# Two graph transformer layers: scores, segment softmax and sums from three blocks into one loop over four chunks

## The chip, the cores and the metric

The kernel runs on one core of a Trainium2 chip. A core has five engines that run their own instruction streams and meet at semaphores: TensorE (PE, matrix products, with weight loads shown apart as PEld), VectorE (DVE), ScalarE (ACT), GpSimd (POOL) and SyncE (SP). The metric is the device time of one execution in microseconds; lower is better.

## The reference, cut to what matters

A graph of N = 3125 nodes and 50000 edges, D = 128 features, passes through a relational layer, a convolution with batch norm, a GATv2 layer with a feed-forward part, and two transformer layers (`L3`). The last two are what the change rebuilds. H = 4 heads of C = 32:

```python
q = (x @ Wq + bq).reshape(N, H, C); k = ...; v = ...
alpha = jnp.einsum('ehc,ehc->eh', q[dst], k[src]) / jnp.sqrt(jnp.float32(C))
amax = jax.ops.segment_max(alpha, dst, num_segments=N)
ealpha = jnp.exp(alpha - amax[dst])
denom = jax.ops.segment_sum(ealpha, dst, num_segments=N)
attn = ealpha / denom[dst]
out = jax.ops.segment_sum(attn[..., None] * v[src], dst, num_segments=N)
return out.reshape(N, H * C) + x @ Ws + bs
```

## The kernel before, in words

The nodes lie in W = 25 windows of Q = 125. An early stage sorts the edges by destination into PAIRS = 416 pairs of a window and a tile of 128 edges, so that all edges of a pair point into one window. G = 4 pairs make a group, 104 groups in all. `pair_src` and `pair_dst` hold source row and place in the window of each edge, `pair_win_i` the window of each pair; TensorE and its weight-load queue read it into registers (line 892) to address `acc` and the PSUM sums.

A transformer layer is a chain of five blocks, and no engine enters a block before all have left the one before:

- `conv_nodes` makes q, k, v and the skip term for all nodes in `acc` and stores k and v to `kv_table` in DRAM.
- `conv_scores` runs over the groups. GpSimd gathers 128 rows of k and v per pair (line 917, eight groups of buffers `got`, one gather per pair). VectorE makes a one-hot of destinations (line 927), TensorE transposes it (line 1801), ScalarE copies it out as `hot_t` (line 1787), TensorE multiplies it with the window's q (line 1814) into one of two banks `q_b`. VectorE multiplies with k (`prod`, line 1775), reduces over a head (`score`, line 1778) and scales into `alpha` (line 1780). SyncE stores the v half to `v_rows`.
- `segment_softmax` takes all 416 x 4 columns of `alpha` at once: transposes, scans for the running maximum of a segment forward and backward, two products that spread a lane's border value, elementwise passes, and the exponential.
- `conv_sums` runs over 52 double groups: rows of v come back from `v_rows`, VectorE makes one-hots (line 1064) and weighted messages (line 1068), TensorE adds them into seven PSUM banks (line 1092), and the denominators from weights split into three bfloat16 parts (line 1093), with a product of zeros after every second pair (line 1097).
- `conv_finish` divides, adds the skip term and, in the last layer, normalises and stores.

Four lines of TensorE's part in conv_scores set its order, a transpose of the next group ahead of this group's products:

```python
turn(1 - b, g + 1)
pe.wait_ge(copied_t, g + 1)
pe.wait_ge(used, g + 1)
for j in range(G):
```

The code as a program prints it, with the line numbers of the profile:

Of the kernel before, what the change touches and what calls it, by code (L numbers as in the profile page):

```python
# [16 lines left out]
ENG = mybir.EngineType  # L17
# [3 lines left out]
Q, W = 125, 25  # L21
P = 128
# [8 lines left out]
YS, Y_EARLY, SL = 6, 6, 24  # L31
# [5 lines left out]
assert TILES * P >= E and FULL + W <= PAIRS and Q * W == N  # L37
# [51 lines left out]

def nodes(ap):  # L90
    return ap.rearrange("(w q) d -> q w d", q=Q)


def segment_softmax(nc, m, acc=None):
# [3 lines left out]
    with ExitStack() as ctx:  # L98
# [12 lines left out]
        alpha = m.alpha[:, :, :].rearrange("l h p -> l (h p)")  # L111
# [34 lines left out]
        def _(dve):  # L146
# [12 lines left out]
            link(v.tensor_copy(topf, high[:, 0:cols]))  # L159
# [18 lines left out]
            link(v.tensor_tensor(less, m.alpha[:, :, :], top[:, :, :], ALU.subtract))  # L178
# [7 lines left out]
def common(m, sb):  # L186
# [14 lines left out]
    m.alpha = sb("alpha", [P, H, PAIRS])  # L201
# [307 lines left out]
def relation_layer(nc, m, y_table):  # L509

    with ExitStack() as ctx:  # L511
# [19 lines left out]
        same = m.alpha  # L531
        pens = m.small[:, :, :].rearrange("l p k -> l (p k)")
        start_pen, end_pen = (pens[:, k * H * PAIRS:(k + 1) * H * PAIRS].rearrange("l (h p) -> l h p", h=H) for k in range(2))
# [32 lines left out]
        def _(dve):  # L566
# [69 lines left out]
            for h in range(H):  # L636
                go(v.tensor_copy(start_pen[:, h, :], ps[2][:, 0:PAIRS]))
                go(v.tensor_copy(end_pen[:, h, :], ps[3][:, 0:PAIRS]))
# [22 lines left out]
            go(v.tensor_scalar(m.leader[:, :], start_pen[:, 0, :], -1.0, None, ALU.is_lt))  # L661
# [69 lines left out]
        def _(pe):  # L731
# [40 lines left out]
            for k, pen in enumerate((start_pen, end_pen)):  # L772
                flat = pen[:, :, :].rearrange("l h p -> l (h p)")
# [61 lines left out]
def gcn_nodes(nc, m, ins, t_table):  # L835

    with ExitStack() as ctx:
# [4 lines left out]
        tb, hb = [bank(f"t1{i}") for i in range(2)], [bank(f"h1{i}") for i in range(4)]  # L842
        loaded, chain, var_ready, std_ready, x_ready = (sem(n) for n in ("loaded1", "chain1", "var1", "std1", "x1_ready"))
# [3 lines left out]
        @block.sync  # L847
        def _(sp):
            sp.dma_start(w1[:, :], ins["L1_gnn_W"]).then_inc(loaded, 16)
            for w in range(0, W, 5):  # L850
                sp.wait_ge(t_ready, w + 5)
                sp.dma_start(nodes(t_table)[:, w:w + 5, :], tmp[:, w:w + 5, :]).then_inc(stored, 16)
            sp.wait_ge(stored, 16 * (W // 5))

# [8 lines left out]

        @block.scalar
        def _(act):
            std_of(nc, act, stats, var_ready, std_ready, 1)
# [6 lines left out]
        def _(pe):  # L873
            pe.wait_ge(x_ready, 1)
# [130 lines left out]


def conv_sums(nc, m, v_rows):


    with ExitStack() as ctx:  # L1010
        sb, sem, bank = scope(nc, ctx)
        zeros = sb("zeros", [P, 512], BF16)
        rows = sb("rows", [P, 2, WG, D])
        hot = sb("hot", [P, 2, WG, Q])
        msg = sb("msg", [P, 2, WG, D])
        wts = sb("wts", [P, 2, WG, H])
        hot_b, wts3 = sb("hot_b", [P, 2, WG, Q], BF16), sb("wts3", [P, 2, WG, 3, H], BF16)
        left, zero = sb("left", [P, 2, WG, H]), sb("zero", [P, WG, H])
        sums = bank("sums", (P, 8 * 512))
        dens = 7 * 512  # L1020
        used, zeroed, done, hot_ready, wts_ready, msg_ready = (sem(n) for n in (
            "used", "zeroed", "all_summed", "hot_ready", "wts_ready", "msg_ready"))
        hot_b_ready, parts_ready, chain, zero_ready = (sem(n) for n in ("hot_b_ready", "parts_ready", "parts_chain", "zero_ready"))
        come = [sem("come0"), sem("come1")]
        steps = PAIRS // (2 * WG)
        block = ctx.enter_context(nc.Block())


        @block.sync
        def _(sp):  # L1030
            with sp.Fori(0, steps) as i:
                for b in range(2):
# [891 lines left out]
```

## Time and profile before

| what | value |
|---|---|
| median of 3 runs | 4879.6 us (4878.93 to 4885.05) |
| the profiled execution's own time | 4863.76 us |
| its span | 4862.0 us, 67990 instructions |
| PE busy | 3211.9 us (66%) |
| DVE busy | 2813.1 us (58%) |
| POOL busy | 2734.6 us (56%) |
| ACT busy | 888.8 us (18%) |
| mean granted clock of TensorE | 0.716 |

The span runs from the first to the last instruction of the program. Busy shares are averages over stages of different limits; the two transformer layers are the last 1700 us or so. The granted clock is given as a share of 2.4 GHz, so 0.50 is the 1.2 GHz level and 1.0 the 2.4 GHz level. The trace shows a float product as two instructions ("halves"), and one matmul of the program's order is two rows' worth of count there.

### The profile page before, as it was taken

What the parts mean: (1) busy time and instruction counts of PE and PEld (TensorE: products, weight loads), DVE (VectorE), ACT (ScalarE), POOL (GpSimd) and SP (SyncE); (2) the same over time, 40 slices, a digit from 0 to 9 for tenths busy, and PEclk for the clock granted to TensorE, in tenths of its full rate; (3) what the DMA queues carried; (4) which work ended last, traced back from release to release, by engine and by line L of the source; (5) the groups of instructions that cost most, each with busy time, mean ns of one, the idle gap of its engine ahead of it and who ended that gap; (6) DMA issues with size and microseconds to landing.
All of it is one profiled execution on the core that took longest, in us unless ns stands there. A gap on an engine that the chain in (4) does not pass through costs nothing. (4 is left out here: it accounts for less than half of the span.)

```text
span 4862.0 us, 67990 instructions
## 1 busy us (share of the span) xinstructions
PE 3211.9 (66%) x15577; PEld 2186.9 (45%) x15578; DVE 2813.1 (58%) x9606; ACT 888.8 (18%) x2002; POOL 2734.6 (56%) x3193
## 2 busy tenths in 40 slices
PE   6766677743433259999996998544443984444395
PEld 3235566633333224555543444434443863444284
DVE  8997454431111586676767888744444663444476
ACT  1000111110000021111114777311110211111021
POOL 0016677327777047555535886067774746777373
PEclk9985555555555579999998999855555995555597
DMA  1111122211111104233321221045553435555342
GB/s 61 39 38 45 43 53 53 26 33 51 50 50 50 31 1 103 77 80 79 78 46 43 67 69 49 15 141 153 152 153 93 142 100 143 153 154 154 87 150 83
DMA packets 320800, 387.80 MB, mean 80 GB/s; under 512 B 45989, under 2 KB 230133, under 8 KB 320618
## 3 DMA queue, kind: packets, MB, share of 16 engines
q0 software_dynamic: 80000, 192.10, 15.7%
q1 hardware_dynamic: 240618, 193.80, 13.2%
q14 instruction: 132, 1.08, 0.1%
q8 instruction: 50, 0.82, 0.1%
HBM read 279.89 MB, written 105.84 MB: 79 GB/s over the span
## 5 line engine op out<-in xcount | busy, mean ns | idle before, releaser
L917 POOL DMA_INDIRECT got<-kv_table,pair_src x832 | 814.9, 979 | 497.5 <-issue 252.9
L559 POOL DMA_INDIRECT y_got<-y_table,y_idx x416 | 399.0, 959 | 505.3 <-SPq L511 338.2
L927 DVE TENSOR_TENSOR hot<-pair_dst,iota 128x500 bf16<-128x500 f32 (+1 forms) x424 | 289.3, 683 | 511.0 <-PE sums L990 474.0
L917 POOL DMA_INDIRECT got<-t_table,pair_src x416 | 414.8, 997 | 267.9 <-ACTq L953 141.5
L917 POOL DMA_INDIRECT got<-x_table,pair_src x420 | 398.3, 948 | 286.2 <-issue 283.3
L1801 PE MATMUL hot_b<-ident_b,hot 128*125 128x128 bf16 x840 | 144.1, 327 | 566.5 <-DVE hot L927 566.4
L1439 DVE SCALAR_TENSOR_TENSOR junk<-z,att 128x128 f32<-128x128 f32 x1664 | 381.4, 287 | 179.1 <-PE z L1497 178.1
L1775 DVE TENSOR_TENSOR prod<-q_b,got 128x512 f32<-128x512 f32 x208 | 143.8, 692 | 570.4 <-DMA got<-kv_table,pair_src 538.8
L1493 PE MATMUL z<-gat_wl,got_t 128*128 128x512 f32 x832 | 432.1, 600 | 0.0
L990 PE MATMUL sums<-got,hot 128*125 128x128 f32 x832 | 214.7, 438 | 328.2 <-DMA got<-t_table,pair_src 328.2
L1202 PE MATMUL sums<-msg,hot 128*125 128x512 f32 x832 | 405.3, 636 | 29.2 <-POOL msg L1143 29.2
L1814 PE MATMUL q_b<-acc,hot_t 125*128 x1664 | 420.1, 434 | 0.1
L1801 PEld LDWEIGHTS hot_b<-ident_b,hot 128*125 128x125 bf16 x840 | 105.2, 217 | 628.5 <-DVE hot L927 628.5
L1814 PEld LDWEIGHTS q_b<-acc,hot_t 125*128 125x128 f32 x1664 | 380.1, 333 | 0.5 <-issue 0.5
L990 PEld LDWEIGHTS sums<-got,hot 128*125 128x125 f32 x832 | 184.3, 326 | 359.1 <-issue 359.1
L1497 PE MATMUL z<-xr,hot_t 125*128 x1248 | 336.1, 377 | 0.0
L1188 DVE TENSOR_TENSOR acc<-acc,sums 125x536 f32 x416 | 295.2, 710 | 52.5 <-PE sums L1206 8.3
L1787 ACT CAST hot_t<-hot_b 125x512 f32<-125x512 bf16 x210 | 123.2, 587 | 1010.3 <-PE hot_b L1801 1010.1
L1092 PE MATMUL sums<-msg,hot 128*125 128x128 f32 x1664 | 301.4, 296 | 5.7
L1092 PEld LDWEIGHTS sums<-msg,hot 128*125 128x125 f32 x1664 | 272.0, 188 | 32.5 <-issue 20.3
L1143 POOL TENSOR_TENSOR msg<-rows,wts 128x512 f32<-128x512 f32 x208 | 247.2, 1207 | 36.3 <-DVE wts L1172 33.4
L683 DVE SCALAR_TENSOR_TENSOR hot_w<-iota,src_loc,psum 128x125 f32<-128x125 f32 x416 | 115.2, 339 | 256.9 <-PE psum L795 256.9
(410 smaller groups left out, 6314.8 us busy)
## 6 DMA issues: line engine op xcount, KB each, us to landing
v_rows<-got SPq DMA_DIRECT2D x208, 256.0 KB, 3.2
rows<-v_rows SPq DMA_DIRECT2D x104, 512.0 KB, 3.7
x_rows<-got SPq DMA_DIRECT2D x104, 256.0 KB, 2.6
rows<-x_rows SPq DMA_DIRECT2D x104, 256.0 KB, 2.6
got<-kv_table,pair_src POOLq DMA_INDIRECT x832, 2.9
y_table<-y_stage SPq DMA_DIRECT2D x25, 500.0 KB
got<-x_table,pair_src POOLq DMA_INDIRECT x420
y_got<-y_table,y_idx POOLq DMA_INDIRECT x416, 2.5
```

Source lines behind the costliest of these rows:

```text
L559: pool.indirect_dma_start(out=got[:, slot, j, :], out_offset=None, in_=y_table[:, :], in_offset=bass.IndirectOffsetOnAxis(ap=m.y_idx[:, co ...
L917: pool.indirect_dma_start(out=self.got[:, slot, j, :], out_offset=None, in_=self.table[:, :], in_offset=bass.IndirectOffsetOnAxis(ap=self. ...
L927: v.tensor_tensor(self.hot[:, b, :, :], bc_last(m.pair_dst[:, cols], Q), bc_mid(m.iota[:, 0:Q], G), ALU.is_equal).then_inc(self.hot_ready, 1)
L990: last = t.matmul(sums[0:Q, bass.ds(ws[j] * D, D)], loop.hot[:, b, j, :], loop.got[:, slot, j, :], start=False, stop=False)
L1092: t.matmul(sums[0:Q, bass.ds(ws[j] * D, D)], hot[:, b, j, :], msg[:, b, j, :], start=False, stop=False)
L1188: v.tensor_tensor(row, row, sums[j][0:Q, 0:H * D + 6 * H], ALU.add).then_inc(read, 1)
L1202: t.matmul(sums[j][0:Q, 0:H * D], hot[:, b, j, :], msg[:, b, j, :], start=True, stop=True)
L1439: last = v.scalar_tensor_tensor(junk[:, j, h, :], z[j][:, h * D:(h + 1) * D], 0.0, m.att[:, h * D:(h + 1) * D], ALU.max, ALU.mult, accum_o ...
L1493: t.matmul(z[j][:, :], got_t[:, b, j, :], m.gat_wl[:, :], start=True, stop=False)
L1497: last = t.matmul(z[j][:, :], hot_t[:, b, j, :], m.xr3[:, bass.ds(ws[j], 1), k, :].rearrange("q o d -> q (o d)"), start=False, stop=(k == 2))
L1801: last = t.transpose(hot_b[b][0:Q, j * P:(j + 1) * P], hot[:, b, j, :], m.ident_b[:, :])
L1814: last = t.matmul(q_b[b][:, j * P:(j + 1) * P], hot_t[:, b, j, :], m.acc[:, bass.ds(w, 1), 0:D].rearrange("q o d -> q (o d)"), start=True, ...
```

## The change

The three blocks `conv_scores`, `segment_softmax` and `conv_sums` of both transformer layers become one block, `conv_layer`. The pairs are cut into four chunks of 128, 128, 96 and 64 (`CHUNK`). For each group of a chunk the scores are made; in chunk c the messages and sums of chunk c - 1 are made beside them (`sums_due` says which: one group of sums per group of scores in chunk 1, 32 over 24 groups in chunk 2, 24 over 16 in chunk 3). At a chunk's end comes a softmax over its own columns. The last chunk's sums follow after the loop. A segment that reaches over a chunk's border is summed into three spare rows (125 to 127) of the PSUM window with the border's own maximum, and at the end scaled by a share and joined by a product (`part`, `rejoin`).

Parts that go with it:

- The transposed one-hot no longer comes from TensorE and ScalarE. `gcn_nodes` writes the destinations once to DRAM as rows (`dst_rows`); ScalarE's queue loads them broadcast (`dst_row`), and VectorE compares them with the lane number (`turn_hot`).
- All seven and a half banks of PSUM hold sums and denominators; q products have one bank, `work`, which the softmax uses too.
- The denominators are float products of four columns with the float one-hot as weights. The three-part split on GpSimd, the bfloat16 copy on ScalarE and the products of zeros are gone.
- The scale of the scores is put into q's weights in `conv_nodes`.
- `alpha` is laid out by chunks, for which `relation_layer`, the softmax of the GAT layer and `gat_scores` (four loops on VectorE instead of one) are adapted. `gcn_nodes` makes the tables of the border rows with some 35 small VectorE instructions.
- The loop is written out for each group on every engine.

The core of the diff:

```diff
-def conv_sums(nc, m, v_rows):
...
+def sums_due(c, k):
+
+    if not c:
+        return ()
+    before, n = groups_of(c - 1), len(groups_of(c))
+    return before[k * len(before) // n:(k + 1) * len(before) // n]
...
+        dens, work = W * D, psum[:, 7 * 512:8 * 512]
...
+            def turn_hot(g):
+                dve.wait_ge(row_in[g % 3], 16 * (g // 3 + 1))
+                if g >= 2:
+                    dve.wait_ge(q_done, g - 1)
+                v.tensor_scalar(hot_t[:, g % 2], dst_row[:, g % 3, :].rearrange("q (w j l) -> q w j l", w=2, j=2), m.lane[0:Q, :], None,
+                                ALU.is_equal).then_inc(hot_t_ready, 1)
+
+            def score(c, g):
+                at = g * G - CHUNK_AT[c]
+                dve.wait_ge(q_done, g + 1)
+                dve.wait_ge(come[g % 8], 16 * G * (g // 8 + 1))
+                v.tensor_tensor(prod[:, g % 2, :, :], work.rearrange("p (j d) -> p j d", j=G), got[:, g % 8, :, 0:D], ALU.mult
+                                ).then_inc(used, 1)
+                if g + 1 < groups:
+                    turn_hot(g + 1)
+                dve.wait_ge(used, g + 1)
+                v.reduce_sum(chunk_view(m.alpha, c)[:, :, at:at + G],
+                             prod[:, g % 2, :, :].rearrange("p j (h c) -> p h j c", h=H), AX).then_inc(scored, 1)
+
+            def messages(s):
...
+                if s >= 2:
+                    dve.wait_ge(summed, s - 1)
+                v.tensor_tensor(hot[:, s % 2],
...
+                dve.wait_ge(row_back[s % 3], 16 * (s // 3 + 1))
+                dve.wait_ge(exped, c + 1)
+                v.tensor_tensor(msg[:, s % 2, :, :].rearrange("l j (h c) -> l j h c", h=H),
+                                rows[:, s % 3, :, :].rearrange("l j (h c) -> l j h c", h=H),
+                                w.rearrange("l h j -> l j h").unsqueeze(3).broadcast_to([P, G, H, C]), ALU.mult).then_inc(msg_ready, 1)
...
+            for c in range(len(CHUNK)):
+                for k, g in enumerate(groups_of(c)):
+                    score(c, g)
+                    for s in sums_due(c, k):
+                        messages(s)
+                softmax(c)
...
         @block.tensor
         def _(pe):
             t = nc.tensor
...
+            def query(c, k, g):
+                ws = windows(nc, m.pair_win_i, ENG.PE, g * G, G)
+                pe.wait_ge(hot_t_ready, g + 1)
+                if g:
+                    pe.wait_ge(used, g)
+                if c and not k:
+                    pe.wait_ge(low_read, c)
                 for j in range(G):
...
+                    last = t.matmul(work[:, j * P:(j + 1) * P], hot_t[:, g % 2, j // 2, j % 2, :],
+                                    m.acc[:, bass.ds(ws[j], 1), 0:D].rearrange("q o d -> q (o d)"), start=True, stop=True)
+                last.then_inc(q_done, 1)
+
+            def add(c, s):
+                ws = windows(nc, m.pair_win_i, ENG.PE, s * G, G)
+                w = wts[:, c % 2, 0:H * CHUNK[c]].rearrange("l (h p) -> l h p", h=H)
+                pe.wait_ge(msg_ready, s + 1)
+                for j in range(G):
+                    t.matmul(psum[:, bass.ds(ws[j] * D, D)], hot[:, s % 2, j // 2, j % 2, :], msg[:, s % 2, j, :], start=False, stop=False)
+                    last = t.matmul(psum[:, bass.ds(ws[j] * H + dens, H)], hot[:, s % 2, j // 2, j % 2, :],
+                                    w[:, :, s * G + j - CHUNK_AT[c]], start=False, stop=False)
+                last.then_inc(summed, 1)
...
+            for c in range(len(CHUNK)):
+                for k, g in enumerate(groups_of(c)):
+                    query(c, k, g)
+                    for s in sums_due(c, k):
+                        add(c - 1, s)
+                softmax(c)
+            for s in groups_of(last_chunk):
+                add(last_chunk, s)
...
         for n, src in ((1, m.x), (2, m.h)):
             conv_nodes(nc, m, ins, n, src, kv_table)
-            conv_scores(nc, m, kv_table, v_rows)
-            segment_softmax(nc, m)
-            conv_sums(nc, m, v_rows)
+            conv_layer(nc, m, kv_table, dst_rows, v_rows)
             conv_finish(nc, m, n == 2, out)
```

On TensorE, in the loop of conv_scores, before (`hot_b` are the transposes of the next group, `q_b_18` this group's q products; ISA rows set an address register):

```order
L892 TENSOR_LOAD pair_win_i
L1799 ISA
L1801 MATMUL hot_b_18<-ident_b,hot 125x128 x4
L1810 REGISTER_ALU
L1814 ISA
L1814 MATMUL q_b_18<-acc,hot_t 128x128
```

And in a group of chunk 1 now (line 1949 adds messages, line 1950 denominators, line 1940 is the query of the next group):

```order
L1949 MATMUL psum<-h,acc 128x128
L1950 ISA
L1950 MATMUL psum<-wts,acc 128x4
L944 TENSOR_LOAD pair_win_i
L1940 ISA
L1940 MATMUL psum<-acc 128x128
```

The adds of one group now stand ahead of the queries of the next in one queue, and the transposes are gone.

On VectorE, in the loop of conv_scores, before:

```order
L1775 TENSOR_TENSOR prod<-q_b_18,got 128x512
L1777 REGISTER_ALU
L1778 TENSOR_REDUCE score<-prod 128x16
L1780 ISA
L1780 TENSOR_SCALAR alpha<-score 128x4x4
L927 ISA
L927 TENSOR_TENSOR hot<-pair_dst,iota 128x500
```

And in a group of chunk 1 now (1808 is prod, 1801 `turn_hot` of the next group, 1813 the reduction, 1824 the one-hot and 1829 the messages of `messages`; `h` and `acc` are the memory that prod, msg and the one-hots are laid in):

```order
L1808 TENSOR_TENSOR h<-psum,got 128x512
L1801 TENSOR_SCALAR acc<-dst_row,lane 125x2x256
L1813 TENSOR_REDUCE alpha<-h 128x4x4
L1824 TENSOR_TENSOR acc<-pair_row,iota 128x2x256
L1829 TENSOR_TENSOR h<-small,wts 128x512
```

Two operations for the sums have come in between the reduction of one group and the product of the next.

## Rows read from the trace of the kernel before

**Rows 1.** The page's second part, 40 slices of the span: PE, granted clock.

```profile
PE   6766677743433259999996998544443984444395
PEclk9985555555555579999998999855555995555597
```

**Rows 2.** Stretches of the program: busy time by engine, instructions, granted clock.

```profile
core 0: us, PE busy (x) PEld busy (x) DVE busy (x) ACT busy (x) POOL busy (x), PEclk, DMA share, GB/s
560.00:990.00 430.00, 312.42 (x1798) 268.64 (x1797) 207.58 (x1052) 68.40 (x181) 263.07 (x279) 0.50 0.20 43
3182.00:3723.00 541.00, 260.53 (x1252) 229.82 (x1252) 231.78 (x417) 61.60 (x105) 409.00 (x416) 0.50 0.55 151
3723.00:3775.00 52.00, 14.07 (x42) 8.87 (x42) 30.76 (x15) 4.34 (x2) 0.00 (x0) 0.60 0.00 0
3776.00:3968.00 192.00, 185.52 (x1488) 169.14 (x1486) 133.50 (x156) 53.32 (x52) 144.02 (x208) 0.99 0.46 142
```

**Rows 3.** Groups in 3182:3723: busy us, mean ns of one, idle before.

```profile
L917 POOL DMA_INDIRECT got<-kv_table,pair_src x416 | 409.4, 984 | 304.1 <-POOLq L55 177.7 <-issue 126.4
L1814 PE MATMUL q_b<-acc,hot_t 125*128 x832 | 210.3, 434 | 0.1
L1775 DVE TENSOR_TENSOR prod<-q_b,got 128x512 f32<-128x512 f32 x104 | 71.9, 691 | 288.0 <-DMA got<-kv_table,pair_src 266.9 <-PE q_b L1814 21.0
L1778 DVE TENSOR_REDUCE score<-prod 128x16 f32<-128x512 f32 x104 | 71.3, 686 | 3.5
L1780 DVE TENSOR_SCALAR alpha<-score 128x16 f32 x104 | 28.7, 276 | 13.6 <-DVE score L1778 2.0
```

**Rows 4.** Timeline: both layers' first gather and last sum; start us, us.

```profile
3181.62 1.02 POOL L917 DMA_INDIRECT got<-kv_table,pair_src  x1 [177.68 <-POOLq L55]
3188.49 0.69 DVE L1775 TENSOR_TENSOR prod<-q_b,got 128x512 f32<-128x512 f32 x1 [5.13 <-DMA got<-kv_table,pair_src]
3968.19 0.46 DVE L1073 TENSOR_REDUCE dens<-sums 125x100 f32<-125x300 f32 x1
4026.21 1.00 POOL L917 DMA_INDIRECT got<-kv_table,pair_src  x1 [66.98 <-POOLq L55]
4809.72 0.46 DVE L1073 TENSOR_REDUCE dens<-sums 125x100 f32<-125x300 f32 x1
```

**Rows 5.** Timeline of TensorE over one group of conv_scores.

```profile
3401.94 0.69 PE L1801 MATMUL hot_b<-ident_b,hot 128*125 128x128 bf16 x4 [2.70 <-DVE hot L927]
3402.42 2.02 PE L1814 MATMUL q_b<-acc,hot_t 125*128 x8
```

**Rows 6.** Groups on VectorE that are nearest to the new operations.

```profile
L1173 DVE TENSOR_TENSOR hot<-pair_dst,iota 128x500 f32<-128x500 f32 x104 | 70.6, 679 | 0.0
L1068 DVE TENSOR_TENSOR msg<-rows,wts 128x1024 f32<-128x1024 f32 x52 | 66.2, 1274 | 2.2 <-DMA rows<-v_rows 2.2
L646 DVE TENSOR_SCALAR first_pen<-alpha 128x416 f32<-128x416 f32 x1 | 0.4, 377 | 0.1
```

**Rows 7.** Timeline of TensorE in gat_nodes: 8 columns, then 512 columns.

```profile
1701.46 9.02 PE L1316 MATMUL g_lin<-w_lin,xt 128*125 128x8 f32 x50 [0.40 <-ACT xt L257]
1739.67 1.12 PE L1322 MATMUL g_l<-gat_wl,xt 128*125 128x512 f32 x2 [2.22 <-DVE z_self L1377]
1743.86 2.07 PE L1322 MATMUL g_l<-gat_wl,xt 128*125 128x512 f32 x2 [1.46 <-DVE z_self L1377]
```

**Rows 8.** Timeline of TensorE in gat_finish, eight halves of 128 columns.

```profile
3028.57 1.04 PE L1567 MATMUL a_o<-gat_wl,agg_t 128*125 128x128 f32 x8
```

**Rows 9.** Timeline of segment_softmax: its first and its last instruction.

```profile
3727.87 3.00 PE L122 MATMUL sg_low<-ident,alpha 128*128 128x128 f32 x13 [13.79 <-PEq L55]
3770.82 3.06 ACT L143 ACTIVATE small<-carried 128x1664 f32<-128x1664 f32 x1 [41.70 <-DVEq L180]
```

**Rows 10.** Timeline: VectorE's last copies and SyncE's stores in gcn_nodes.

```profile
1028.24 5.53 DVE L862 COPY gcn_h<-h 125x128 f32<-125x128 f32 x25 [6.91 <-PE h L881]
1030.16 11.18 SPq L852 DMA_DIRECT2D t_table<-tmp  x5
```

More of the change, by code:

```diff
@@ L36 @@
 BLOCKS = H * PAIRS // P
-assert TILES * P >= E and FULL + W <= PAIRS and Q * W == N
+CHUNK = (128, 128, 96, 64)
+CHUNK_AT = tuple(sum(CHUNK[:c]) for c in range(len(CHUNK)))
+assert TILES * P >= E and FULL + W <= PAIRS and Q * W == N and sum(CHUNK) == PAIRS and all(n % 32 == 0 for n in CHUNK)
 PHASE = itertools.count()
@@ L1728, in _ @@
             dve.wait_ge(loaded, 128)
+            nc.vector.tensor_scalar(w4[:, 0, :], w4[:, 0, :], float(C) ** -0.5, None, ALU.mult)
+            nc.vector.tensor_scalar(b4[:, 0, :], b4[:, 0, :], float(C) ** -0.5, None, ALU.mult).then_inc(scaled, 1)
+            dve.wait_ge(scaled, 1)
             for w in range(W):
@@ new lines, in _, with load @@
+            for slot in range(8):
+                pool.wait_ge(come[slot], 16 * G * (groups // 8))
+        @block.sync
+        def _(sp):
+            loaded = 0
+            def load(s):
+                sp.wait_ge(aside[s % 8], 16 * (s // 8 + 1))
+                if s >= 3:
+                    sp.wait_ge(msg_ready, s - 2)
+                sp.dma_start(rows[:, s % 3, :, :], v_rows[s, :, :].rearrange("l (j d) -> l j d", j=G)).then_inc(row_back[s % 3], 16)
+            for c in range(len(CHUNK)):
+                for k, g in enumerate(groups_of(c)):
+                    sp.wait_ge(come[g % 8], 16 * G * (g // 8 + 1))
+                    sp.dma_start(v_rows[g, :, :].rearrange("l (j d) -> l j d", j=G), got[:, g % 8, :, D:2 * D]
+                                 ).then_inc(aside[g % 8], 16)
+                    if c:
+                        due = sums_due(c, k)
+                        ahead = min(due.stop + 2 if len(due) else loaded, groups_of(c - 1).stop)
+                        while loaded < ahead:
+                            load(loaded)
+                            loaded += 1
+            while loaded < groups:
+                load(loaded)
+                loaded += 1
@@ new lines, in _ @@
+            v.memset(zeros[:, :], 0.0).then_inc(zeroed, 1)
+            turn_hot(0)
+            for c in range(len(CHUNK)):
+                for k, g in enumerate(groups_of(c)):
[3 more added lines that the diff above has]
+                softmax(c)
+            for b in (1, 0):
+                link(v.tensor_scalar(share[:, b, :], firsts[:, b + 1, :], m.span_pen[:, b:b + 1], None, ALU.add))
+                link(v.tensor_tensor(firsts[:, b, :], firsts[:, b, :], share[:, b, :], ALU.max))
@@ L1819, in conv_finish @@
+            for k in range(7):
+                last = t.matmul(psum[:, k * 512:(k + 1) * 512], zeros[:, 0:P], zeros[:, :], start=False, stop=True)
+            last.then_inc(closed, 1)
+            pe.wait_ge(parts_ready, last_chunk)
+            for b in range(last_chunk):
+                last = t.matmul(work[0:Q, b * (D + H):(b + 1) * (D + H)], m.rejoin[:, b, :], part[:, b, :], start=True, stop=True)
+            last.then_inc(rejoined, 1)
 def conv_finish(nc, m, last_layer, out):
```

423 lines of the change are left out of this document (241 added, 182 removed).

## The prediction

> **What bounds the kernel now.** I read the page's slices first: TensorE is 40 to 90% busy almost everywhere, but its granted clock is 5 tenths (the 1.2 GHz level) in most slices in which it works in short bursts [rows 1]. The stretches come next [rows 2]. A transformer layer has three blocks: conv_scores (541 us), segment_softmax (52 us), conv_sums (192 us). From a layer's first gather to its last sum they take 3181.6 to 3968.65 = 787.0 us, and 4026.2 to 4810.2 = 784.0 us in the second layer [rows 4].
>
> The groups of conv_scores show its bound [rows 3]: 416 gathers of 984 ns each plus 126.4 us of issue gaps, 535.8 us, so 5.15 us for the four pairs of a group. VectorE waits 266.9 us for the gathers and only 21.0 us for TensorE. TensorE has 2.02 us of q products in a group behind 0.5 us of transposes [rows 5], all at clock 0.50. In conv_sums TensorE is busy 185.5 of 192 us at clock 0.99 [rows 2]. The idea of the change is to do these 192 us beside the gathers. The question is whether a group then still takes 5.15 us.
>
> **The new loop is a ring.** The printed order says on TensorE: `add` of group s, then `query` of group g+1; on VectorE: `score` of g, then `messages` of s. `add(s)` waits for `msg_ready`, which `messages(s)` raises; that stands behind `score(g)` on VectorE, which waits for `q_done` of `query(g)`; and `query(g+1)` stands behind `add(s)` on TensorE. Nothing overlaps: the time of a group is VectorE's five operations plus TensorE's add plus TensorE's query. Before, each of these ran beside the gathers or beside each other, with two q banks; `work` is one bank now.
>
> VectorE's part, D. prod 0.69 and reduce 0.69 [rows 3]; the one-hot of 512 columns 0.69, from 679 ns for 500 [rows 6]; the message product of 512, 0.69 (half of 1274 is 0.64 [rows 6]; the 512-column product of rows 3 takes 0.69). `turn_hot` has no row: its nearest is the float tensor_scalar of 416 columns at 377 ns, 0.46 for 512 [rows 6], and 16 columns beside the gathers take 276 ns on average [rows 3], which looks like waiting; I take 0.50, with 0.46 and 0.66 as ends. With 0.24 for six hand-overs (the idle before L1778 is 3.5/104 = 0.03, taken as 0.04): D = 3.26 + 0.24 = 3.5 us.
>
> TensorE's query, Q: eight halves of 128 float columns, 2.02 + 0.03 = 2.05 us at clock 0.50 [rows 5]; the halves are (2.02 - 0.42)/7 = 0.23 us apart.
>
> TensorE's add, A: four message products of two halves, 8 x 0.23 = 1.84. The denominators are now float products of 4 columns with a float one-hot as weights, two halves each. Their nearest row is g_lin, 8 float columns: 50 halves in 9.02 us, 0.178 apart, weight load included [rows 7]. 8 x 0.178 = 1.42. A = 1.84 + 1.42 + 0.05 = 3.3 us at 1.2 GHz. Ends: the denominators free behind the messages (A = 1.9), or as dear as messages (8 x 0.25, A = 3.9).
>
> Trainium skill, "TensorE: Matmul & The Clock Gate", on LDWEIGHTS, gives a weight load as the number of columns over 1.2 GHz, some 0.107 us for 128, whatever the rows hold. By it the denominators' halves would be 0.107 apart, A would be 2.75 and the forecast below about 115 us lower, an estimate from that page. The rows of g_lin (0.178) disagree and I follow them.
>
> **Which clock.** A and Q double at 1.2 GHz, so this decides the sign. Three rows speak for the low level: in the relation layer TensorE is busy 312 of 430 us (73%), in bursts with gaps, at clock 0.50; in conv_scores 260 of 541 at 0.50 [rows 2]; and g_lin's narrow products keep TensorE busy for 9.02 us without a gap, and still at the slow level, 0.178 apart from first to last [rows 7]. The new loop has the same make-up: narrow products for 1.4 of 3.3 us, and a gap of 3.5 us in every 8.85. conv_sums kept 0.99 [rows 2] with a 512-column product of zeros after every second pair (line 1097); those are gone. Against: gat_nodes, with wide products and 2.2 us gaps, swings between the levels (the same pair of halves takes 1.12 and 2.07 us [rows 7]). I take 1.2 GHz throughout.
>
> **The sum of one layer.** A group with one add is D + A + Q = 8.85 us, longer than the gathers' 5.15, so gathers, stores and loads of rows hide, and every stop of VectorE counts.
> - Chunk 0, no sums: 6.9 us to the first product [rows 4], 31 x 5.15, 1.9 for the last score: 168.4.
> - Chunk 1, 32 groups with one add: 32 x (3.5 + 3.3) + 31 x 2.05 = 281.2.
> - Chunk 2, 24 groups, 32 adds: 24 x 6.8 + 23 x 2.05 + 8 x 3.3 = 236.8 (a second message hides beside the first add).
> - Chunk 3, 16 groups, 24 adds: 16 x 6.8 + 15 x 2.05 + 8 x 3.3 = 166.0.
> - Four softmaxes. The old one takes 3727.87 to 3770.82 = 43 us for 1664 columns [rows 9]. By columns 512, 512, 384 and 256 cost 13.2, 13.2, 9.9 and 6.6; about 4 us each for some 25 short instructions and ten hand-overs are my estimate (0 and 8 are the ends): 59. While one runs no group is scored; the first query of the next chunk hides in it, which is why 31, 23 and 15 queries stand above. Only the first could use gathers that run ahead, and the chunk after it is not bound by gathers, so none is hidden.
> - The end: shares 1.5, first message 1.5, 16 x 3.3 = 52.8, closing products 3, parts 1.5, copies 3.5 and border rows 1.2: 65.0.
>
> Together 976 us against 787.0 and 784.0: +189 and +192. Elsewhere: about 35 short VectorE instructions in gcn_nodes, some 7.5 us by estimate, of which SyncE's stores, ending at 1041.3 against the copies' 1033.8 [rows 10], cover most; 0.6 us per layer for the scaled q weights; three more loop starts in gat_scores, where TensorE is the bound. I take +7 for all, 0 to 12. The scaling instruction per group goes, but it lay beside the gathers and is worth nothing.
>
> 4863.8 (the profiled execution) + 381 + 7 = 5252. The median of the runs is 4879.6, 16 more, so 5268; I say 5265, +7.9%.
>
> **The rivals.**
> - *The clock rises in the loop* (faster). A = 8 x 0.11 + 8 x 0.09 = 1.6 and Q = 1.1, from 8 halves in 1.04 us, (1.04 - 0.27)/7 = 0.11 apart [rows 8], and half of 0.178. Chunks 168.4 + 197.3 + 160.5 + 110.9, softmaxes 48, end 36: 721 a layer, -128 in all, 4759 against the median. It needs fast products through gaps of 3.5 us; gat_nodes does that part of the time with gaps of 2.2 [rows 7]. The point of change: with D = 3.5 a layer breaks even at A + Q of about 3.3, where 5.35 stands in the sum. 9%.
> - *The clock swings* as in gat_nodes: half-way between, 5015. The adds and the query that follows are one burst of 5.35 us, longer than any in conv_scores, which speaks for it. 14%.
> - *The change does what its name says*, sums wholly beside gathers: 168.4 + 72 x 5.15 + 10.6 + 65 = 615 a layer, 4545. It would need queries to be issued ahead of adds, and the printed order shows the reverse. 1%.
> - *VectorE takes time from the gathers*: `turn_hot` may block GpSimd. One slowed gather a group, 0.5 us x 31 in chunk 0 of both layers, +31 at most; later gathers have 3.7 us to spare.
>
> Behind that last one stands a rule. The Trainium skill, "SBUF — State Buffer", on the shared port pair, says that a VectorE operation in a two-port mode, tensor_scalar among them, locks GpSimd out of writing descriptors. By it up to the same 31 us would come on top; no row separates it here.
>
> **How the numbers follow.** Low clock 73% (5265; its own range by the ends of A, 208 adds x -1.4 or +0.6, is 4975 to 5390, with 30 us more for `turn_hot`, softmaxes and gathers), swinging 14%, high 9%, wholly hidden 1%, some other 3%. The lower end of A is as unlikely as the swinging case is low, so 5020 to 5430 leaves about 2 in 10 out. No change means within 0.2%, about 10 us, which is what a measurement of this kernel can tell. Faster 10%, the same 2%, slower 88%.
>
> **What would show it.** Right: in chunks 1 to 3 granted clock 0.50 to 0.55; VectorE idle about 5.3 us in a group, released by q's products; POOL idle far over the issue gaps; 8.8 us from prod to prod; the four-column halves 0.18 apart. Wrong: clock near 0.9 there and a group of 6.2 us, or products of `query` that start while `add`'s messages are still being made.

## The result, and the profile of the changed kernel

The changed kernel takes 5248.79 us (median of 4 runs, 5246.51 to 5254.31). The kernel before took 4879.27 us beside it. The ratio is 1.0757, with a 95% interval of 1.0738 to 1.0775. The forecast was 5265.

The page of the changed kernel, its slices for TensorE and the granted clock, and three groups:

```profile
PE   6766777533332589999699954466667644666674
PEclk9975555555555799999899986555555555555555
...
L1754 POOL DMA_INDIRECT got<-kv_table,pair_src x832 | 849.4, 1021 | 1156.0 <-DVE h L1808 530.4
L1949 PE MATMUL psum<-h,acc 128*128 128x128 f32 x1664 | 646.9, 493 | 475.2 <-DVE h L1829 475.2
L1808 DVE TENSOR_TENSOR h<-psum,got 128x512 f32<-128x512 f32 x208 | 143.8, 691 | 1063.7 <-PE psum L1940 845.0
```

In [rows 1] each transformer layer ended in slices of clock 0.9, those of conv_sums. They are gone: from slice 26 on all is 0.5, with TensorE 40 to 70% busy. The idle columns show who waits for whom, here over both layers. The gathers wait 530 us for the scores, the sums 475 us for VectorE's messages, the scores 845 us for the queries, some 422 us in each layer. In [rows 3], which is one layer, the scores waited 21 us for TensorE and 267 us for the gathers.

Stretches of the first layer, one in each chunk and one in the last block of sums:

```profile
core 0: us, PE busy (x) PEld busy (x) DVE busy (x) ACT busy (x) POOL busy (x), PEclk, DMA share, GB/s
3210.00:3365.00 155.00, 62.99 (x245) 54.09 (x244) 50.87 (x90) 0.00 (x0) 117.53 (x124) 0.51 0.68 181
3400.00:3640.00 240.00, 153.56 (x672) 145.44 (x672) 81.43 (x142) 0.00 (x0) 129.70 (x124) 0.50 0.51 147
3690.00:3890.00 200.00, 136.23 (x605) 130.43 (x605) 68.48 (x119) 0.00 (x0) 90.28 (x84) 0.50 0.45 131
3940.00:4070.00 130.00, 93.30 (x419) 89.82 (x417) 41.77 (x72) 0.00 (x0) 27.25 (x26) 0.50 0.37 106
4105.00:4150.00 45.00, 45.00 (x211) 45.00 (x212) 16.81 (x26) 0.00 (x0) 0.00 (x0) 0.50 0.24 74
```

The first gather and the last instruction of both layers, from the timeline (start us, us):

```profile
3205.54 0.99 POOL L1754 DMA_INDIRECT got<-kv_table,pair_src  x1 [182.22 <-POOLq L57]
...
4169.26 0.15 DVE L1909 TENSOR_TENSOR dens<-dens,psum 125x4 f32 x1
...
4229.23 0.95 POOL L1754 DMA_INDIRECT got<-kv_table,pair_src  x1 [226.12 <-POOLq L57]
...
5194.79 0.15 DVE L1909 TENSOR_TENSOR dens<-dens,psum 125x4 f32 x1
```

So a layer takes 4169.41 - 3205.54 = 963.9 and 5194.94 - 4229.23 = 965.7 us, against 787.0 and 784.0 [rows 4]. The forecast was 976. From the starts of L1808 over each chunk, a group takes 5.06 us in chunk 0, 8.55 in chunk 1, 9.58 in chunk 2 and 10.14 in chunk 3. From the start of the last score to the layer's end it is 90.5 us.

One group of chunk 1 on all engines, from the timeline:

```profile
3407.70 0.69 DVE L1808 TENSOR_TENSOR h<-psum,got 128x512 f32<-128x512 f32 x1 [5.67 <-PE psum L1940]
...
3408.31 0.48 DVE L1801 TENSOR_SCALAR acc<-dst_row,lane 125x512 f32<-125x512 bf16 x1
3408.70 0.68 DVE L1813 TENSOR_REDUCE alpha<-h 128x16 f32<-128x512 f32 x1
...
3409.30 0.68 DVE L1824 TENSOR_TENSOR acc<-pair_row,iota 128x512 f32<-128x512 f32 x1
...
3409.90 0.69 DVE L1829 TENSOR_TENSOR h<-small,wts 128x512 f32<-128x512 f32 x1
...
3410.73 0.79 PE L1949 MATMUL psum<-h,acc 128*128 128x128 f32 x2 [3.06 <-DVE h L1829]
...
3411.53 0.55 PEld L1949 LDWEIGHTS psum<-h,acc 128*128 128x128 f32 x2
...
3411.96 0.55 PEld L1950 LDWEIGHTS psum<-wts,acc 128*128 128x128 f32 x2
...
3412.38 0.55 PEld L1949 LDWEIGHTS psum<-h,acc 128*128 128x128 f32 x2
...
3414.16 2.06 PE L1940 MATMUL psum<-acc 125*128 x8
...
3416.25 0.69 DVE L1808 TENSOR_TENSOR h<-psum,got 128x512 f32<-128x512 f32 x1 [5.67 <-PE psum L1940]
```

This is the ring. VectorE's five operations last from 3407.70 to 3410.73 (D = 3.03) while TensorE is idle. The sums last to 3414.16 (A = 3.43) and the query to the next score at 3416.25 (Q = 2.09), while VectorE is idle for 5.67 us. No piece lies beside another: 3.03 + 3.43 + 2.09 = 8.55. The sums are sixteen halves, so 3.43 / 16 = 0.214 us for each. The weight loads show both kinds: from a message product (L1949) to the denominators' product (L1950) it is 0.43 us, and from there to the next message product 0.42 us, two halves each time. A half costs the same whether it moves 128 columns or four.

### The profile page after: what moved, and what is told of

Same layout as the page of the kernel before. It is cut to its first block and busy times, and to the rows that moved or that the text cites. A ratio compares the mean times of both kernels' runs of the same rounds, so it can differ in the third digit from the quotient of the medians.

```text
span 5248.5 us, 62934 instructions
## 1 busy us (share of the span) xinstructions
PE 3492.5 (67%) x15135; PEld 2474.7 (47%) x15140; DVE 2722.8 (52%) x9731; ACT 658.1 (13%) x1697; POOL 2492.8 (47%) x2775
## 3 DMA queue, kind: packets, MB, share of 16 engines
q14 instruction: 144, 1.18, 0.1%
## 5 line engine op out<-in xcount | busy, mean ns | idle before, releaser
L1754 POOL DMA_INDIRECT got<-kv_table,pair_src x832 | 849.4, 1021 | 1156.0 <-DVE h L1808 530.4
L1949 PE MATMUL psum<-h,acc 128*128 128x128 f32 x1664 | 646.9, 493 | 475.2 <-DVE h L1829 475.2
L1808 DVE TENSOR_TENSOR h<-psum,got 128x512 f32<-128x512 f32 x208 | 143.8, 691 | 1063.7 <-PE psum L1940 845.0
L1949 PEld LDWEIGHTS psum<-h,acc 128*128 128x128 f32 x1664 | 448.1, 329 | 518.4 <-issue 518.4
L1940 PE MATMUL psum<-acc 125*128 x1664 | 428.4, 439 | 198.8 <-DVE acc L1801 189.2
L1940 PEld LDWEIGHTS psum<-acc 125*128 125x128 f32 x1664 | 376.7, 331 | 227.1 <-issue 227.1
L1950 PEld LDWEIGHTS psum<-wts,acc 128*128 128x128 f32 x1664 | 454.9, 333 | 0.0
L979 DVE TENSOR_TENSOR hot<-pair_dst,iota 128x500 f32<-128x500 f32 (+1 forms) x212 | 144.7, 683 | 493.4 <-PE sums L1042 488.2
L1950 PE MATMUL psum<-wts,acc 128*128 128x4 f32 x1664 | 355.8, 284 | 0.0
L1117 ACT ACTIVATE msg<-rows,wts 128x128 f32<-128x128 f32 x832 | 254.1, 388 | 1.4 <-DMA rows<-x_rows 1.4
```

The costliest lines, as they stand in the source:

```text
L1754: pool.indirect_dma_start(out=got[:, slot, j, :], out_offset=None, in_=kv_table[:, :], in_offset=bass.IndirectOffsetOnAxis(ap=m.pair_src[: ...
L1940: last = t.matmul(work[:, j * P:(j + 1) * P], hot_t[:, g % 2, j // 2, j % 2, :], m.acc[:, bass.ds(ws[j], 1), 0:D].rearrange("q o d -> q (o ...
L1949: t.matmul(psum[:, bass.ds(ws[j] * D, D)], hot[:, s % 2, j // 2, j % 2, :], msg[:, s % 2, j, :], start=False, stop=False)
L1950: last = t.matmul(psum[:, bass.ds(ws[j] * H + dens, H)], hot[:, s % 2, j // 2, j % 2, :], w[:, :, s * G + j - CHUNK_AT[c]], start=False, s ...
```

## The experiments

Two theories stand against each other. **The ring**: the loss comes from the order, in which TensorE's next query stands behind sums that wait for VectorE. **The clock**: the loss comes from TensorE at the 1.2 GHz level alone, and the order matters little. A third question is what the float denominators cost. The kernels ran on three chips, named here by what the kernel before takes on them: 4878.49, 4862.3 and 5385.03 us. Ratios are against the kernel before on the same chip, and layers are compared by their length in the trace. On the 5385 us chip the changed kernel itself was not run, and the times expected there (4815, 4750, 4950 and 4500 to 4560 us) were worked out for a chip like the first, so that none of them was met.

**The same two kernels again.** The changed kernel and the kernel before, both unaltered, on the 4878 us chip:

> The changed kernel unaltered, as the standard for the runs beside it. The four kernels before this one were timed on a chip on which the kernel before takes 5385 us instead of 4879. If that chip comes again: slow stretches are in the written-out code (stops of some 2 us in every eight gathers, 10 us on VectorE), so the changed kernel, written out in full, should be well over its 5249, about 5620 (4 percent above the kernel before), and e1_ahead's 5266 a gain over it of some 300 us. If a chip like the first comes: 5249.

> The kernel before unaltered, for its trace on this chip. If the slow stretches belong to written-out code, conv_scores and conv_sums on TensorE and VectorE, which are loops, keep their own times and only GpSimd's written-out gathers are slower; if the memory is slower, the gathers' time to landing grows.

5249.13 us (5246.14 to 5253.77), ratio 1.0762 (1.0744 to 1.078), and 4877.52 us in one run. The loss repeats. This run of the kernel before also settles a side question. In the changed kernel's profile the first gather of the transformer layers stands at 3205.54, 23.9 us later than in [rows 4]. In this second profile of the kernel before, the same gather reads (timeline):

```profile
3201.04 1.02 POOL L917 DMA_INDIRECT got<-kv_table,pair_src  x1 [177.63 <-POOLq L55]
```

So 19.4 of the 23.9 us also come between two profiles of the unaltered kernel. The 4.5 us that are left are hardly clear of the scatter: on this one chip the gather stands at 3203.69, 3205.73 and 3206.77 us in three profiles of kernels whose code up to there is the changed kernel's.

**The next query ahead of the sums**, the direct test of the ring. VectorE's work and every product stay:

```diff
-                    query(c, k, g)
+                    if not k:
+                        query(c, k, g)
+                    if g + 1 in groups_of(c):
+                        query(c, k + 1, g + 1)
                     for s in sums_due(c, k):
                         add(c - 1, s)
```

> TensorE issues the query of group g+1 ahead of the adds that go with group g; nothing else moves. Ring theory: VectorE's 3.03 us (first product to first add) no longer stand in series with TensorE's 3.43 + 2.09, so a group of chunks 1 to 3 takes the 5.5 us of TensorE instead of 8.55, 72 groups x 3.03 x 2 layers = 436 us less, about 4815 us, granted clock still 0.50. If TensorE without a gap is also given the high clock, groups are bound by the gathers at 5.15 or less: 4740 us or below. If the loop is slow for another reason (written-out code, contention of the row loads), the order changes little: over 5150 us.

> e1_ahead again, beside the changed kernel itself. Ring theory: a group of chunks 1 to 3 from 8.55 to 5.5 us, 436 us less than the changed kernel on the same chip where nothing else stops the engines (about 4815 against 5249); with the stops of the other chip at least 250 us less. Rival: under 100 us less.

On the 5385 us chip: 5266.39 us, ratio 0.9777 (0.9761 to 0.9793), a layer 811.1 and 810.2 us. On the 4878 us chip: 4765.27 us (4763.76 to 4766.2), ratio 0.9768 (0.9751 to 0.9784), a layer 721.4 and 723.5 us. It is the same gain over the kernel before on two chips far apart. On the second it is 484 us less than the unaltered changed kernel beside it, where 436 were expected. A timeline of chunk 1 and stretches of chunks 1, 2 and 3 of the second run:

```profile
3409.07 2.05 PE L1940 MATMUL psum<-acc 125*128 x8
...
3410.92 0.64 PE L1949 MATMUL psum<-h,acc 128*128 128x128 f32 x2
...
3411.16 0.69 DVE L1808 TENSOR_TENSOR h<-psum,got 128x512 f32<-128x512 f32 x1 [2.24 <-PE psum L1940]
```

```profile
3372.00:3530.00 158.00, 148.84 (x679) 145.00 (x680) 92.62 (x164) 0.63 (x1) 122.37 (x118) 0.50 0.79 221
...
3580.00:3700.00 120.00, 120.00 (x565) 120.00 (x564) 66.03 (x111) 0.00 (x0) 85.78 (x84) 0.50 0.74 213
3740.00:3830.00 90.00, 90.00 (x424) 90.00 (x423) 48.48 (x82) 0.00 (x0) 30.82 (x30) 0.50 0.56 162
```

The next sums start at 3410.92, ahead of the score at 3411.16: TensorE no longer stops. A group falls from 8.55, 9.58 and 10.14 us to 5.06, 6.08 and 6.60. In chunk 1 that is TensorE's 24 halves of 0.21 us without a gap, 5.1 us, where the expectation had 5.5 from A + Q. It is by chance as long as four gathers take, but VectorE waits for queries there and not for gathers. In chunks 2 and 3 TensorE is busy for all of 120 and 90 us, and it is the bound there too. All of this at a granted clock of 0.50. The order alone is worth the 484 us.

**Products of zeros behind the query**, the test of the clock. The ring stays; twelve bfloat16 products of zeros (512 columns) in chunks 1 to 3 keep TensorE busy while VectorE works:

```diff
                     query(c, k, g)
+                    for _ in range(12 if c else 0):
+                        t.matmul(psum[:, 0:512], zeros[:, 0:P], zeros[:, :], start=False, stop=False)
```

> The changed kernel with twelve products of zeros (512 columns, bfloat16, adding zero to the first bank) between query and adds in chunks 1 to 3, where TensorE otherwise waits. It tells what the clock is worth with the ring in place. If the clock rises: A from 3.43 to about 1.7, Q from 2.09 to 1.1, fillers 12 x 0.213 = 2.6 us inside the gap of 3.03; a group takes 5.8 us, total 72 x 2 x 2.7 + 32 x 2 x 1.7 = 500 us less, about 4750. If it does not rise, the fillers take 5.1 us each time, 2.1 us more than the gap: about 5550.

> The changed kernel with 12 products of zeros (bf16, 512 columns) behind each query in chunks 1 to 3; the ring of sums, query, score and messages is kept. It asks how much of the loss is the clock alone. With the sums ahead of the zeros TensorE would show a granted clock near 1.0 instead of 0.50 in these chunks, the four sums of a group would take 1.8 us instead of 3.4 and the query 1.1 instead of 2.1. If the ring sets the pace, each group of chunk 1 takes 8.55 - 1.6 - 1.0 = 5.9 us, and in chunks 2 and 3, with a third and a half more sums per group, 6.5 and 6.9: 85 + 75 + 52 = 210 us less per layer, 4830 us in all (4760 to 4900). If the clock stays at 0.50 behind zeros, the zeros hang behind the query without effect and the time stays at 5249, or rises if the next sums must wait for the zeros. On another chip it took 5277 us where the kernel before took 5385.

On the 5385 us chip: 5277.19 us, ratio 0.9805 (0.9784 to 0.9827). On the 4862 us chip: 4821.95 us (4811.13 to 4824.69), ratio 0.991 (0.9897 to 0.9924), a layer 758.3 and 760.1 us, a group 6.08, 6.65 and 6.83 us. Chunk 1 and the last block of sums of that run:

```profile
3376.00:3560.00 184.00, 169.29 (x1075) 119.21 (x1091) 86.58 (x151) 0.00 (x0) 139.66 (x136) 0.98 0.72 206
...
3890.00:3935.00 45.00, 45.00 (x213) 45.00 (x212) 16.27 (x26) 0.00 (x0) 0.00 (x0) 0.50 0.20 59
```

The clock is 0.98 where zeros stand among the narrow products. It is 0.50 in the last block, where TensorE is busy without a gap in the same narrow float products alone. By the timeline of that group A falls to 1.80 us and Q to 1.18, and D stays at 3.02, as the sum has it. The clock alone, at its high level, would have been enough to turn the change into a small gain, but the ring still costs: with it, at the high clock, a layer takes 37 us more than without it at the low one.

**Without the denominators.** The 1664 four-column products are left out, and each denominator is taken as at least 1.0:

```diff
-                    last = t.matmul(psum[:, bass.ds(ws[j] * H + dens, H)], hot[:, s % 2, j // 2, j % 2, :],
-                                    w[:, :, s * G + j - CHUNK_AT[c]], start=False, stop=False)
```

> Leaves out the four-column products that add the denominators (the denominators are then 1), everything else as in the changed kernel. Theory of the sum: the eight halves of an add cost 8 x 0.178 = 1.42 us in series, 208 adds, 296 us less: about 4950. If they are hidden behind the message products, no difference; by one half per load at 0.107 us, 178 us less, 5070.

> The changed kernel without the 416 pairs' products of four columns that sum the denominators (1664 of them; the denominators are then taken as at least 1.0, so the outputs are not the reference's). It asks what the denominators cost in the ring. If the ring sets the pace at the lower clock, a group of sums takes 3.43 - 4 x 0.43 = 1.7 us instead of 3.4, of which 208 groups carry it on the path: 1.7 x 208 = 355 us less at most; 1.43 us per group, as forecast in the sum (0.36 us for each four-column product), gives 297 us less. Forecast 4930 (4890 to 4960). If the denominators hide behind VectorE's hot and message operations, less than 100 us.

On the 5385 us chip: 5296.59 us, ratio 0.9836 (0.9819 to 0.9852). On the 4862 us chip: 4837.95 us (4836.55 to 4842.74), ratio 0.995 (0.9936 to 0.9963), a layer 768.7 and 767.7 us. That is lower than the 4890 to 4960 expected. Stretches of chunks 1 and 2 and of the last block:

```profile
3376.00:3580.00 204.00, 112.06 (x480) 103.34 (x479) 86.56 (x150) 0.00 (x0) 139.15 (x133) 0.51 0.64 183
3607.00:3770.00 163.00, 92.95 (x420) 87.43 (x421) 74.44 (x129) 0.20 (x1) 98.25 (x92) 0.63 0.62 177
3925.00:3955.00 30.00, 21.51 (x132) 17.86 (x131) 23.02 (x41) 0.00 (x0) 0.00 (x0) 0.84 0.36 104
```

A group of chunk 1 falls from 8.55 to 6.82 us: eight halves of 0.214 us, 1.71. The forecast had priced them at 1.42. The rest comes with the clock: without the four-column products it reads 0.63 in chunk 2 and 0.84 in the last block, with TensorE less busy than before (93 of 163 us in chunk 2), and the last block falls from 90.5 to 52.7 us. So a four-column product costs as much as one of 128 columns, and without these products the clock no longer stays at 0.50 after chunk 1. In chunk 1 it still reads 0.51 with the same products, so their width alone does not settle the clock.

**The sums in one block.** All sums of a chunk stand ahead of the second group's query of the next, instead of beside its gathers:

```diff
-    return before[k * len(before) // n:(k + 1) * len(before) // n]
+    return () if k else before
```

> The changed kernel, but all the sums of a chunk are made in one block ahead of the second group's query of the next chunk, instead of spread beside its gathers. It asks what the spreading gives. In the block a group of sums takes 3.43 us (as in the tail after the last chunk), 88 of them per layer before the tail: 302 us. Beside the block and the softmax ahead of it only 8 groups of gathers fit in the buffers; these 8 then pass at TensorE's and VectorE's pace of some 3.6 us, the others at the gathers' 5.05. Chunk 1: 32 x 3.43 + 8 x 3.6 + 24 x 5.05 = 260 us (265 to 274 as spread), chunk 2 110 + 29 + 81 = 220 (230), chunk 3 82 + 29 + 40 = 151 (162). So, if the ring of the spread form is as serial as the forecast has it, the block costs nothing: 5210 us (5170 to 5260). If spreading does hide sums beside gathers, the block is slower by what it hides: 5350 or more.

5044.0 us (5041.98 to 5050.49) beside 4862.3, ratio 1.0374 (1.036 to 1.0388), a layer 870.4 and 868.7 us: 94 and 97 us less than as spread. The expectation had 5210 us (5170 to 5260), some 39 us less for both layers together, and missed. From the timeline, the block and the groups behind it:

```profile
3386.57 0.69 DVE L1824 TENSOR_TENSOR acc<-pair_row,iota 128x512 f32<-128x512 f32 x1 [2.12 <-PE psum L1950]
...
3389.98 0.69 DVE L1824 TENSOR_TENSOR acc<-pair_row,iota 128x512 f32<-128x512 f32 x1 [2.12 <-PE psum L1950]
...
3490.88 0.69 DVE L1808 TENSOR_TENSOR h<-psum,got 128x512 f32<-128x512 f32 x1 [7.45 <-PE psum L1940]
...
3552.25 0.69 DVE L1808 TENSOR_TENSOR h<-psum,got 128x512 f32<-128x512 f32 x1 [1.66 <-PE psum L1940]
```

In the block a group of sums takes 3.41 us, TensorE's own time, since VectorE makes the messages one group ahead. Behind it the groups pass in 3.41 us (18 of them from 3490.88 to 3552.25), and only the last 11 at 5.4 us, waiting for gathers. The expectation let only the 8 buffered groups pass so fast. But the gathers go on meanwhile, so more than twice as many profit: from the first score behind the block to the last it is 121 us. Chunk 1 takes 235 us in place of 265. The spread form as built is therefore slower than a block beside which no group is scored.

**Both cures at once**, the query ahead of the sums, and six products of zeros between them:

```diff
                     if g + 1 in groups_of(c):
                         query(c, k + 1, g + 1)
+                    for _ in range(6 if c else 0):
+                        t.matmul(psum[:, 0:512], zeros[:, 0:P], zeros[:, :], start=False, stop=False)
```

> Query ahead as in e1_ahead, and six products of zeros between it and the adds in chunks 1 to 3. If ring and clock are the two causes, a group falls to the gathers' 5.15 us, the softmaxes are partly made up by gathers that run ahead: about 4500 to 4560, below both kernels. If only the ring matters, the fillers cost 6 x 0.43 in a TensorE-bound loop: e1_ahead's time plus 370 us.

> e4_ahead_fill again, beside the changed kernel. On a chip without the stops: granted clock above 0.8 in chunks 1 to 3, groups at the gathers' 5.1 us, about 4550. With them: within 1 percent of e1b_ahead, since what stops the engines then is neither ring nor clock.

On the 5385 us chip: 5242.51 us, ratio 0.9731 (0.9711 to 0.975). On the 4878 us chip: 4618.35 us (4614.33 to 4621.55), ratio 0.9465 (0.9449 to 0.9481), a layer 647.5 and 650.1 us, a group 4.86, 4.58 and 4.85 us. That is 68 us more than the 4550 expected; the last block still takes some 88 us. Stretches of chunks 1 to 3, and the gathers and the scores in 3400 to 3520 (chunk 1):

```profile
3372.00:3530.00 158.00, 128.23 (x872) 103.03 (x873) 97.50 (x170) 0.63 (x1) 122.06 (x119) 0.90 0.78 222
3580.00:3660.00 80.00, 80.00 (x620) 68.98 (x619) 58.18 (x99) 0.00 (x0) 61.72 (x61) 1.00 0.91 264
3700.00:3760.00 60.00, 60.00 (x473) 52.41 (x472) 43.19 (x73) 0.00 (x0) 39.96 (x40) 1.00 0.86 247
...
L1754 POOL DMA_INDIRECT got<-kv_table,pair_src x91 | 93.7, 1030 | 27.7 <-issue 26.2 <-DVE h L1808 1.5
L1808 DVE TENSOR_TENSOR h<-psum,got 128x512 f32<-128x512 f32 x25 | 17.3, 691 | 47.3 <-DMA got<-kv_table,pair_src 36.0 <-PE psum L1940 11.3
```

Without zeros TensorE is busy for 120 of 120 us at clock 0.50 (1.2 GHz); with them for 80 of 80 us at 1.00 (2.4 GHz). The pair has the same chunk and the same busy share, and differs in the products. GpSimd now gathers with no stop but its issue gaps up to the layer's last gather. In chunk 1 VectorE waits mostly for gathers (36.0 of 47.3 us). In chunks 2 and 3 it waits only for TensorE, because the groups gathered during the softmaxes are still in the buffers. This beats the kernel before by 5.3%.

**Zeros in chunk 0 and in the last block too**, six and three per group:

```diff
-                    for _ in range(6 if c else 0):
+                    for _ in range(6):
...
             for s in groups_of(last_chunk):
                 add(last_chunk, s)
+                for _ in range(3):
+                    t.matmul(psum[:, 0:512], zeros[:, 0:P], zeros[:, :], start=False, stop=False)
```

> The fastest form so far (the next query issued ahead of a group's sums, 6 products of zeros behind it in chunks 1 to 3; 4618 us), with the 6 products of zeros in chunk 0 too and 3 behind each group of sums in the last block. It asks what bounds chunk 0 and the tail. If chunk 0 is bound by GpSimd's gathers (4 of about 1.0 us with 0.3 us between: 5.05 us per group), it stays at 5.05 per group however high the clock; only the first softmax and the first groups of chunk 1 gain, some 5 to 10 us per layer. The tail's 16 groups take 3.4 us at clock 0.50 and about 2.4 with zeros at 1.0: 16 us less per layer. Forecast 4618 - 2 x 20 = 4578 (4560 to 4615). If chunk 0 were bound by the query or VectorE, it would come out 30 us per layer lower than that.

4583.54 us (4571.57 to 4603.48) beside 4862.3, within the range expected, ratio 0.9426 (0.9404 to 0.9447). Chunk 0 and the last block of the first layer, and the last block of the second:

```profile
3210.00:3350.00 140.00, 87.43 (x385) 49.82 (x392) 47.54 (x84) 0.00 (x0) 105.97 (x112) 0.83 0.70 182
...
3775.00:3810.00 35.00, 34.61 (x224) 30.86 (x227) 14.76 (x23) 0.00 (x0) 0.00 (x0) 0.78 0.30 83
...
4480.00:4530.00 50.00, 49.21 (x217) 42.75 (x219) 15.51 (x24) 0.00 (x0) 0.00 (x0) 0.53 0.19 53
```

In chunk 0 the clock reads 0.83 and a group still takes 5.04 us: the gathers are its bound. Three zeros a group are too few for the last block: its clock rises in one layer (636.5 us) and hardly in the other (658.9). On average a layer takes 647.7 us in this profile, as in the form above (648.8). The profile comes from one of the two longest of the five executions (4601.33 us). By the medians the form is 0.4% better than the one above, each against the kernel before on its own chip, and the two intervals do not meet. Where that gain comes from no trace shows.

## Why the forecast held, step by step

- *The ring* was the right mechanism. Its three pieces add up to 8.55 us where 8.85 stood, and one reordering on TensorE takes the whole loss away. So does the high clock with the ring in place (4822 us): the loss needs both, and the sum had both.
- *D* was too large: 3.5 against 3.03. The operations last what their rows said (0.69, 0.48, 0.68, 0.68, 0.69, in all 3.22), but they start about 0.6 us apart. Each begins 0.08 us before the modelled end of the one ahead; none of the five reads the result of the one just ahead of it. Where an operation does, it starts 0.04 us after that end, as the two scans below. Of the 0.24 us added for hand-overs only the one to TensorE shows, 0.14 us (3409.90 + 0.69 to 3410.73).
- *A* was too small, 3.3 against 3.43, by two errors that cancel in part: the message halves 0.214 apart in place of 0.23, the four-column halves 0.214 in place of 0.178. The row of g_lin [rows 7] was not near enough. *Q* was 2.05 against 2.09.
- *The clock* stayed at 0.50 in chunks 1 to 3, as taken. The reason given was g_lin's row [rows 7], narrow products at the low level without a gap. The runs agree: 0.50 in 120 of 120 busy us of narrow float products, 0.98 to 1.00 with products of zeros among them.
- *The layer*: chunk 0's last score begins after 164.9 us, for 166.5 in the sum. From there to chunk 1's first score it is 20.2 us, for 19.1 (17.2 of softmax, 1.9 of score). The last block, from the last score on, takes 90.5 us. Two of the softmax's scans on VectorE, from the timeline:

```profile
3373.30 1.22 DVE L1839 TENSOR_TENSOR_SCAN small<-start_turned,psum 128x512 f32<-128x512 f32 x1 [1.21 <-PE psum L1959]
3374.56 1.22 DVE L1840 TENSOR_TENSOR_SCAN small<-end_turned,small 128x512 f32<-128x512 f32 x1
```

  The second reads what the first writes, and they start 1.26 us apart. Together a layer takes 964 and 966 us for 976. D had 0.47 x 72 = 34 us too much; A lacked 0.13 x 104 = 14 and Q 3; some 5 us are the softmaxes' and the end's.
- *Elsewhere* +7 was forecast. The second profile of the kernel before leaves 4.5 us for the change up to the first layer; between the layers it is 2.3 us more than in the first profile, behind the second 1.8. That is some 8 us, with a scatter of a few us.
- *Luck.* The errors of D and A have opposite signs, 34 against 14 us a layer. And the sum for the profiled execution, 5252 against 5250.18 us, came out closer than it should: the two layers took 358.6 us more and not 381, and the 19.4 us by which the first gather moves without the change filled the gap. By the medians the forecast lay 16 us over.
- *The rivals.* The clock did not swing: it read 0.50 in every stretch of chunks 1 to 3. A clock that rises did not come by itself; forced by zeros it gave 4822 us beside 4862, where its sum said 4759 against 4880. Its group of chunk 1 was worked out with A + Q = 2.7; measured, 6.08 - 3.03 = 3.05, and the last block stayed at the low clock. Sums wholly beside the gathers needed another order, as said; with it and zeros a layer takes 648 us for the 615 of that sum. `turn_hot` does hold gathers up, but by little. One group of chunk 0, and one of conv_scores in the kernel before, from the timelines:

```profile
3239.66 0.48 DVE L1801 TENSOR_SCALAR acc<-dst_row,lane 125x512 f32<-125x512 bf16 x1
3239.81 1.14 POOL L1754 DMA_INDIRECT got<-kv_table,pair_src  x1 [0.30 <-issue]
...
3308.75 0.68 DVE L927 TENSOR_TENSOR hot<-pair_dst,iota 128x500 bf16<-128x500 f32 x1 [0.25 <-issue]
3308.81 1.44 POOL L917 DMA_INDIRECT got<-kv_table,pair_src  x1 [0.30 <-issue]
```

  A gather takes 0.95 us. One that starts inside `turn_hot` ends about 0.81 us after the end of `turn_hot`, so this one takes 1.14 us; only those that start within its first 0.03 us are not held. In chunk 0 of the first layer 18 gathers start inside it and take 1.04 us on average, under 2 us in all. In the kernel before the one-hot of line 927 did the same, and it is longer: 99 gathers started inside it and took 1.10 us on average, the others 0.95. So a group takes 5.06 us now and 5.15 before, because chunk 0 has no such one-hot beside its gathers. In the form with both cures, where one-hots and messages stand beside them, a gather takes 1.03 us on average. The Trainium skill, "SBUF — State Buffer", "SBUF: two separate sides", on the shared port pair, says that a VectorE operation in a two-port mode locks GpSimd out of writing descriptors. The trace does not say in which mode `turn_hot` runs, but it shows gathers held up by it, by at most 0.25 us each in place of the 0.5 us that the rival took.
- The Trainium skill, "TensorE: Matmul & The Clock Gate", on LDWEIGHTS, gives some 0.107 us for a load of 128 columns. Here the traces agree at the 2.4 GHz level only. At clock 0.98, in the run with twelve products of zeros, the timeline of the sums reads:

```profile
3451.28 0.47 PE L1949 MATMUL psum<-h,acc 128*128 128x128 f32 x2
...
3451.73 0.47 PE L1949 MATMUL psum<-h,acc 128*128 128x128 f32 x2
```

  These are 0.45 us apart with four halves between them, 0.112 each. At 1.2 GHz it is 0.214, and the forecast lay 16 us over the time and not 100 under it because it followed the row.

## What to carry to other kernels

Before work is put beside other work on an in-order engine, write down for each engine which instruction stands behind which wait. If A on one engine waits for B on another, and B's input stands behind A, nothing overlaps, and a plain block of the same work can be faster (5044 against 5249 us). Issue the producer of the next step ahead of the consumer of this one: one call in the program replaced by two, each behind a condition, was worth 484 us. Price narrow float products by the half, not by the column, and look at the granted clock of rows with the same kinds of products: a few wide products among them bought another 3%.

## What the runs showed of the hardware beyond the forecast

One chip took 5385.03 us (5377.4 to 5391.62, 7 runs) for the kernel that takes 4862 to 4879 on the others. Engines stopped there at regular places. In the relation layer the gathers of the form with the query ahead read there (timeline of GpSimd):

```profile
630.97 0.94 POOL L572 DMA_INDIRECT y_got<-y_table,y_idx  x1 [0.30 <-issue]
633.84 0.94 POOL L572 DMA_INDIRECT y_got<-y_table,y_idx  x1 [1.93 <-remote]
```

After every eight gathers GpSimd stops for 1.93 us, where the same kernel on the 4878 us chip shows 0.30 before 408 of these 416 gathers. What it waits for the trace does not say. Whether only written-out code stops so is open too: the chip did not come again when the kernel before was profiled for this question. On this chip the form with both cures gains 2.7% where it gains 5.3% elsewhere. And the gathers of `gcn_sums`, the same code, take 997 ns in one profile of the kernel before and 1040 ns in the other, 17.8 us in 416 of them. Some 17 us of it are gathers that start inside VectorE's one-hot (line 927): 83 at 1.21 us in the one profile, 99 at 1.34 us in the other, while all others take 0.94 to 0.95 us in both. The same operations only met at other moments. A difference of that size in a stage that a change does not touch is no effect of the change.
